# Layer normalisation over channels on partitions: GpSimd adds the channel halves and the halves of the squares, and the mean squares are kept as eight rows of 128 tokens in batches of two groups

## What is computed

```python
def _ln_t(v, eps=1e-05):
    m = jnp.mean(v, axis=-1, keepdims=True)
    s = jnp.var(v, axis=-1, keepdims=True)
    return (v - m) / jnp.sqrt(s + eps)

def layer_norm(x, g, b):
    m = jnp.mean(x, axis=-1, keepdims=True)
    v = jnp.mean(jnp.square(x - m), axis=-1, keepdims=True)
    return (x - m) * jax.lax.rsqrt(v + EPS) * g + b
```

## Time and profile before

| | |
|---|---|
| time before, median of 3 runs | 5374.98 us (5358.56 to 5387.59) |
| profiled execution, its own time | 5375.21 us |
| its span, first to last instruction | 5373.4 us |
| mean granted TensorE clock over the span | 0.892 of full speed |
| busy: TensorE matmul, VectorE, ScalarE, GpSimd | 84%, 55%, 40%, 15% |
| the seven normalisation stages together | 337.90 us |

### The profile page before, as it was taken

How to read it: one execution, slowest core, us unless ns; L and a number is a source line. 1 busy time by engine, 2 the same in 40 slices (tenths; PEclk the granted TensorE clock), 3 DMA queues, 4 the chain that set the end, 5 groups by cost and what they waited for, 6 DMA issues and landing times. The chain is left out here.

```text
span 5373.4 us, 139944 instructions
## 1 busy us (share of the span) xinstructions
PE 4530.5 (84%) x57100; PEld 2834.8 (53%) x57101; DVE 2972.1 (55%) x5849; ACT 2152.0 (40%) x4091; POOL 831.7 (15%) x2139
## 2 busy tenths in 40 slices
PE   3679898887997888897688886799999999984995
PEld 1237777773436777774355554354454545433663
DVE  3444444453024544454488886488686877852343
ACT  1133223232123333331466664277575766721221
POOL 0000000000000000000355553011111111104012
PEclk7788878798998988898899998899999999985997
DMA  1000000000000000000100000000000000006123
GB/s 42 2 7 3 3 3 3 3 3 18 0 0 9 4 3 3 3 4 3 38 1 1 1 1 0 10 1 1 1 0 1 0 1 1 0 3 217 61 84 101
DMA packets 47552, 85.70 MB, mean 16 GB/s; under 512 B 7121, under 2 KB 38129, under 8 KB 46065
## 3 DMA queue, kind: packets, MB, share of 16 engines
q1 hardware_dynamic: 40944, 61.84, 3.3%
q0 software_dynamic: 6144, 16.79, 1.0%
HBM read 45.05 MB, written 33.55 MB: 15 GB/s over the span
## 5 line engine op out<-in xcount | busy, mean ns | idle before, releaser
L1775 PE MATMUL psum<-hm_ex,hm_mix 128*128 128x512 f32 x1024 | 510.4, 621 | 42.3 <-ACT hm_Aq L1855 38.3
L1841 ACT ACTIVATE hm_ex<-psum,hm_nm 128x1024 f32<-128x1024 f32 x256 | 285.6, 1116 | 299.4 <-DVE hm_nm L1899 299.4
L1775 PEld LDWEIGHTS psum<-hm_ex,hm_mix 128*128 128x128 f32 x1024 | 175.6, 191 | 352.5 <-issue 344.8
L1914 DVE COPY hm_A<-psum 128x1024 f32<-128x1024 f32 x256 | 312.9, 1222 | 51.5 <-PE psum L1784 47.9
L1909 DVE TENSOR_SCALAR_CACHE_REDUCE hm_plus<-hm_Aq,hm_cbcol,hm_sums 128x1024 f32<-128x1024 f32 x256 | 340.5, 1330 | 0.0
L1899 DVE TENSOR_REDUCE hm_nm<-psum 128x1 f32<-128x1024 f32 x256 | 311.0, 1215 | 13.5 <-PE psum L1763 13.5
L1784 PEld LDWEIGHTS psum<-K,hm_Aq 128*128 128x128 f32 x2048 | 236.6, 140 | 150.0 <-issue 145.4
L957 DVE TENSOR_TENSOR fw_M<-fw_M,psum 128x256 f32<-128x256 f32 x256 | 107.8, 421 | 348.1 <-PE psum L728 345.6
L1846 ACT ACTIVATE hm_junk<-hm_Aq 128x1024 f32<-128x1024 f32 x256 | 270.6, 1057 | 30.3
L1763 PE MATMUL psum<-hm_kt,hm_qd 64*32 64x512 f32 x4096 | 280.1, 606 | 0.0
L1321 ACT ACTIVATE pt_signs<-pt_acts,pt_tb 128x1024 f32<-128x1024 f32 (+1 forms) x224 | 227.6, 1018 | 116.1 <-POOL pt_tb L1188 95.0
(11 more groups left out here) (379 smaller groups left out, 9044.6 us busy)
## 6 DMA issues: line engine op xcount, KB each, us to landing
ex_rows_in<-ex_zero SPq DMA_DIRECT2D x2, 5120.0 KB, 24.8
ex_xs<-ex_rows_in SPq DMA_DIRECT2D x80, 128.0 KB
ex_rows_out<-ex_ys SPq DMA_DIRECT2D x80, 128.0 KB, 1.7
ex_w<-in_ex_w SPq DMA_DIRECT2D x2, 4096.0 KB
X<-in_x SPq DMA_DIRECT2D x2, 2048.0 KB, 12.5
out_y<-X SPq DMA_DIRECT2D x2, 2048.0 KB, 9.0
ff_w<-in_ff_w SPq DMA_DIRECT2D x2, 1024.0 KB, 5.8
pt_w_proc<-in_pt_proc SPq DMA_DIRECT2D x1, 2048.0 KB, 7.6
```

Source lines behind the costliest of these rows:

```text
L1775: mm = pe.matmul(bank[4 + c], mix[:, u, :], ex[:, u, 512 * c:512 * c + 512], start=True, stop=True)
L1841: act.activation(ex[:, u, :], flat2(psum[:, 2 * u:2 * u + 2, :]), ACT.Exp, bias=nm[:, u:u + 1], accum_out=rsum[:, u:u + 1]).then_inc(s_ex, 1)
L1914: dve.tensor_copy(A[:, :, :, QT_ * t:QT_ * t + QT_], flat2(psum[:, 6:8, :]).rearrange("p (m g n) -> p m g n", m=MT, g=HEADS)).then_inc(s_a ...
```

## The change

GpSimd gets two lists of additions. `sum_halves(g)` adds the two channel halves of the source into one of two buffers `halves`, and `sum_squares(g)` adds the two halves of the squares into one of two buffers `sqs`. TensorE then needs one matmul of 512 columns for a mean instead of two. The mean squares are laid out otherwise: a batch is two groups, 1024 tokens, as a tile of eight rows by 128 tokens. `squares(g)` is four matmuls of 128 columns with weights of eight columns, `spread(g)` four matmuls of 128 columns, each copying one row, and root and reciprocal work on [8, 128] tiles, four times a stage. The lists of all engines become one pipeline over t: group t is centred, t - 2 has its squares summed, t - 4 is spread and scaled. `sq` has two buffers instead of three. The numbers computed are the same up to rounding.

```diff
@@ -338,67 +338,89 @@
     nc = k.nc
-    HALF = NG // 2
+    PARTS = GROUP // P
+    PAIRS = NG // 2
+    ROWS = 2 * PARTS
     with ExitStack() as ctx:
-        sq = k.sb(f"{name}_sq", [P, 3, CH, GROUP], ctx)
-        std = k.sb(f"{name}_std", [HALF, 2, GROUP], ctx)
-        rstd = k.sb(f"{name}_rstd", [HALF, 2, GROUP], ctx)
-        eps = k.sb(f"{name}_eps", [P, 1], ctx)
-        pick = k.sb(f"{name}_pick", [P, 2 * HALF - 1], ctx)
-        s_zero, s_eps, s_mean, s_cen, s_sq, s_msq, s_std, s_rstd, s_bc, s_out, s_shift = (
-            k.sem(f"s_{name}_{n}") for n in "zero eps mean cen sq msq std rstd bc out shift".split())
+        sb = lambda n, s: k.sb(f"{name}_{n}", s, ctx)
+        halves = sb("halves", [P, 2, GROUP])
+        sq = sb("sq", [P, 2, CH, GROUP])
+        sqs = sb("sqs", [P, 2, GROUP])
+        std = sb("std", [ROWS, PAIRS, P])
+        rstd = sb("rstd", [ROWS, PAIRS, P])
+        pick = sb("pick", [P, 2 * ROWS - 1])
+        eps = sb("eps", [P, 1])
+        s_zero, s_eps, s_halves, s_mean, s_cen, s_sq, s_sqs, s_msq, s_std, s_rstd, s_bc, s_out, s_shift = (
+            k.sem(f"s_{name}_{n}") for n in "zero eps halves mean cen sq sqs msq std rstd bc out shift".split())
         bank = k.bank
...
             def _(pool):
+                def sum_halves(g):
+                    if g >= 2:
+                        pool.wait_ge(s_mean, g - 1)
+                    pool.tensor_tensor(halves[:, g % 2, :], at(src, g)[:, 0, :], at(src, g)[:, 1, :],
+                                       ALU.add).then_inc(s_halves, 1)
+
+                def sum_squares(g):
+                    pool.wait_ge(s_sq, g + 1)
+                    if g >= 2:
+                        pool.wait_ge(s_msq, g - 1)
+                    pool.tensor_tensor(sqs[:, g % 2, :], sq[:, g % 2, 0, :], sq[:, g % 2, 1, :],
+                                       ALU.add).then_inc(s_sqs, 1)
+
                 pool.memset(eps[:, :], EPS)
                 pool.memset(pick[:, :], 0.0).then_inc(s_zero, 1)
                 pool.wait_ge(s_zero, 1)
-                pool.memset(pick[:, HALF - 1:HALF], 1.0 / C).then_inc(s_eps, 1)
+                pool.memset(pick[:, ROWS - 1:ROWS], 1.0 / C).then_inc(s_eps, 1)
+                sum_halves(0)
+                sum_halves(1)
+                for g in range(NG):
+                    if g + 2 < NG:
+                        sum_halves(g + 2)
+                    sum_squares(g)
 
             @block.tensor
             def _(pe):
                 def mean(g):
+                    pe.wait_ge(s_halves, g + 1)
                     if g >= 3:
                         pe.wait_ge(s_cen, g - 2)
-                    for h in range(CH):
-                        mm = pe.matmul(bank[g % 3], k.const("ones"), src[:, h, GROUP * g:GROUP * g + GROUP],
-                                       start=(h == 0), stop=(h == CH - 1))
-                    mm.then_inc(s_mean, 1)
+                    pe.matmul(bank[g % 3], k.const("ones"), halves[:, g % 2, :], start=True, stop=True).then_inc(s_mean, 1)
 
                 def squares(g):
-                    pe.wait_ge(s_sq, g + 1)
-                    r = g % HALF
-                    for h in range(CH):
-                        mm = pe.matmul(bank[3 + g // HALF][0:HALF, :], pick[:, HALF - 1 - r:2 * HALF - 1 - r],
-                                       sq[:, g % 3, h, :], start=(r == 0 and h == 0),
-                                       stop=(r == HALF - 1 and h == CH - 1))
+                    pe.wait_ge(s_sqs, g + 1)
+                    if g >= 4 and g % 2 == 0:
+                        pe.wait_ge(s_std, g // 2 - 1)
+                    for q in range(PARTS):
+                        r = PARTS * (g % 2) + q
+                        mm = pe.matmul(bank[3 + g // 2 % 2][0:ROWS, 0:P], pick[:, ROWS - 1 - r:2 * ROWS - 1 - r],
+                                       sqs[:, g % 2, P * q:P * q + P], start=(r == 0), stop=(r == ROWS - 1))
                     mm.then_inc(s_msq, 1)
 
                 def spread(g):
-                    pe.wait_ge(s_rstd, g // HALF + 1)
+                    pe.wait_ge(s_rstd, g // 2 + 1)
                     if g >= 3:
                         pe.wait_ge(s_out, g - 2)
-                    r = g % HALF
-                    pe.matmul(bank[5 + g % 3], k.const("ident")[0:HALF, r:r + 1].broadcast_to([HALF, P]),
-                              rstd[:, g // HALF, :], start=True, stop=True).then_inc(s_bc, 1)
-
-                mean(0)
-                mean(1)
+                    for q in range(PARTS):
+                        r = PARTS * (g % 2) + q
+                        mm = pe.matmul(bank[5 + g % 3][:, P * q:P * q + P],
+                                       k.const("ident")[0:ROWS, r:r + 1].broadcast_to([ROWS, P]), rstd[:, g // 2, :],
+                                       start=True, stop=True)
+                    mm.then_inc(s_bc, 1)
+
                 pe.wait_ge(s_eps, 1)
-                for g in range(HALF):
-                    mean(g + 2)
-                    squares(g)
-                mean(6)
-                mean(7)
-                for g in range(HALF):
-                    squares(HALF + g)
-                    spread(g)
-                for g in range(HALF):
-                    spread(HALF + g)
+                for t in range(NG + 4):
+                    if t < NG:
+                        mean(t)
+                    if 0 <= t - 2 < NG:
+                        squares(t - 2)
+                    if 0 <= t - 4 < NG:
+                        spread(t - 4)
...
                 def square(g):
                     act.wait_ge(s_cen, g + 1)
-                    if g >= 3:
-                        act.wait_ge(s_msq, g - 2)
-                    act.activation(sq[:, g % 3, :, :], at(dst, g), ACT.Square).then_inc(s_sq, 1)
+                    if g >= 2:
+                        act.wait_ge(s_sqs, g - 1)
+                    act.activation(sq[:, g % 2, :, :], at(dst, g), ACT.Square).then_inc(s_sq, 1)
 
                 def root(b):
-                    act.wait_ge(s_msq, HALF * b + HALF)
-                    act.activation(std[:, b, :], bank[3 + b][0:HALF, :], ACT.Sqrt,
-                                   bias=eps[0:HALF, :]).then_inc(s_std, 1)
+                    act.wait_ge(s_msq, 2 * b + 2)
+                    act.activation(std[:, b, :], bank[3 + b % 2][0:ROWS, 0:P], ACT.Sqrt,
+                                   bias=eps[0:ROWS, :]).then_inc(s_std, 1)
...
-                for g in range(HALF + 1):
-                    square(g)
-                root(0)
-                for g in range(HALF + 1, NG):
-                    square(g)
-                root(1)
-                for g in range(NG):
-                    move(g)
+                for t in range(NG + 5):
+                    if t < NG:
+                        square(t)
+                    if t >= 3 and t % 2 == 1 and t // 2 <= PAIRS:
+                        root(t // 2 - 1)
+                    if 0 <= t - 5 < NG:
+                        move(t - 5)
...
                 def scale(g):
                     dve.wait_ge(s_bc, g + 1)
-                    dve.wait_ge(s_cen, g + 1)
+                    dve.wait_ge(s_sq, g + 1)
...
-                for g in range(HALF + 2):
-                    centre(g)
-                invert(0)
-                centre(6)
-                centre(7)
-                for g in range(HALF):
-                    scale(g)
-                invert(1)
-                for g in range(HALF, NG):
-                    scale(g)
+                for t in range(NG + 4):
+                    if t < NG:
+                        centre(t)
+                    if t >= 3 and t % 2 == 1 and t // 2 <= PAIRS:
+                        invert(t // 2 - 1)
+                    if 0 <= t - 4 < NG:
+                        scale(t - 4)
                 dve.wait_ge(s_out, NG)
```

## The result

The changed kernel takes 5393.4 us (median of 20 runs, 5360.1 to 5424.2) against 5362.3 of the kernel before on the same chip (20 runs, 5338.2 to 5394.5): ratio 1.0049, 95% interval 1.003 to 1.0069. The forecast of 5311 us and its range are missed on the slow side. The profiled execution took 5396.4 us, its span is 5394.6.

A forecast was written before the change was run, and what follows sets the result against it. TensorE was taken to bound each normalisation stage. From 5375.2 us, 66.7 saved over the seven stages came off and 2.5 for the configuration load was added, giving 5311 us, range 5280 to 5358.

The forecast's parts named there:

- So a microsecond taken from a stage is one off the total: Seven normalisation stages, 337.90 us together: nothing else runs in them and each ends at a barrier, so savings count fully.
- the last subtraction: Whole kernel: 5375.2 us less 66.7 saved in the seven normalisations, plus 2.5 for the configuration load, gives 5311.
- or if the next stages' lengths change too: Stages behind the normalisations: a change in their lengths was listed as a sign that the prediction is wrong.
- GpSimd's addition: Normalisation stages: each of GpSimd's sixteen additions of 512 columns was priced at 1.26 us.
- The cycle of 3.0: Middle of a normalisation stage: TensorE and VectorE set 3.0 us a group, GpSimd needing 2.5.
- the tail: End of a normalisation stage, after group 7 is summed: last squares, root, reciprocal, spreads and multiplication at half clock, 11.0 us.
- the rival of a tail at full clock: End of a normalisation stage: the clock also stays up there, 3.5 us off a stage, total 5287; chance 0.10.
- The configuration load: Start of ln2: a one-time load now stands ahead of GpSimd's first sum, priced at 2.5 us.
- Half clock in the middle: Normalisation stages: TensorE's clock stays at half, total 5387; chance 0.10 in all stages, 0.08 in some.
- Additions of 1.9: Normalisation stages: each GpSimd addition takes 1.9 us, 3.7 more a stage, total 5337; chance 0.10.
- Mutual blocking: Normalisation stages: GpSimd and VectorE keep each other out, about 56 us a stage, total 5433; chance 0.04.
- The search: Lookup stage: different rounding sets its flag, calling the eighth normalisation and a search, more than 38 us; chance 0.02.

The follow-up runs named there:

- e1_trim: The changed kernel with 8 redundant TensorE waits a normalisation stage left out, putting the fast-weight stages at their old block places; 5285.5 us, ratio 0.983.
- e12_flat: e1_trim with padding matmuls, TensorE's fast-weight loop written out in full and four repeated matmuls in one product of each tile; 5056.6 us, ratio 0.946.
- e5_pad: e1_trim with 16 one-column matmuls after the convolution stage's last matmul and 8 ahead of the feed-forward stage's first wait; 5260.1 us, ratio 0.990.
- e10_bpad: The kernel before with 54 one-column matmuls after the convolution stage's last matmul and 4 ahead of the feed-forward stage's first wait; 5239.6 us, ratio 0.982.

## Why the prediction was wrong

**The step that failed** is "So a microsecond taken from a stage is one off the total", and with it the last subtraction, 5375.2 less 66.7. It holds for the barriers and not for the program's text: 136 more TensorE instructions in each stage shifted everything behind them against the 256-instruction blocks, and the two fast-weight stretches grew by 111.2 us. The text named the sign ("or if the next stages' lengths change too") and no mechanism; none of the rivals was this one. With the true saving, 5375.2 - 86.8 would be 5288, and e1_trim, with that saving (its seven stages are 252.0 us) and the old places, measured 5285.5 (four runs, 5268.9 to 5327.0, on a chip where the kernel before took 5370.8). That the two agree within 3 us is in part luck.

**The prices, term by term.** GpSimd's addition: 1.26 us forecast, 1.267 and 1.268 measured (L373, L366). The reciprocal of [8, 128]: 0.95, measured 0.941. First subtraction 3.8 us into ln2: 201.15 - 197.31 = 3.8. The squares of group 3 summed at 15.0: 14.9. The cycle of 3.0: L393 starts at 211.98, 215.09 and 218.20, so 3.1. Group 7 summed at 27.0: 26.3. The mis-sized term is the tail, 11.0 against 8.5 (26.3 to 34.86): squares(7) and a spread still ran on full clock, which fell at 226.6 only. ln2 by clock:

```profile
197.31:202.00 4.69, 2.94 (x4) 1.12 (x4) 0.85 (x1) 0.20 (x1) 3.53 (x6) 0.50 0.00 0
202.00:226.60 24.60, 21.62 (x125) 12.73 (x124) 17.42 (x17) 9.56 (x12) 16.53 (x14) 0.99 0.00 1
226.60:232.17 5.57, 4.04 (x18) 3.48 (x17) 4.00 (x4) 0.00 (x0) 0.00 (x0) 0.50 0.00 0
```

That is between the forecast and the rival of a tail at full clock. Over the seven stages the sum was 20.1 us short: 9.4 in ln2, ln3 and ln4 (38.0 forecast; 34.9, 35.0 and 34.8 measured), 2.1 in ln5, 8.6 in the stages with gain (40.0 forecast; 38.0, 37.1 and 36.4 measured), which were not taken apart. The configuration load, priced at 2.5, cost nothing to be seen: it stands at 197.6 and the first addition starts at 197.67.

**The rivals.** Half clock in the middle: 0.99 there, so no. Additions of 1.9: no. Mutual blocking: VectorE's L462 takes 1.204 us beside GpSimd, 1.208 before; no. The search: the eighth normalisation does not show among the stages.

## What to carry to other kernels

A change that adds or removes instructions on an engine with a long loop moves all code behind it against the instruction blocks, so compare the stages that the diff does not touch, tile by tile, before judging it by the total. Look for idle time put down to "issue" that stands at the same record of every pass: here it drifted by a fixed count from pass to pass, as a block boundary does, and redundant waits or a few tiny matmuls moved it to a place where it cost nothing. Try an edit at two places within a block, or its worth (here the 86.8 us of the normalisations, 1.6%) can read as nothing.

## What the runs showed that was not expected

- The late block stops TensorE for about 1 to 2 us, a jump back in its loop for about 3 to 7. Where half clock follows, it holds for 3 to 24 us of the tile and costs more than the stop: the tile with the jump takes 30 to 35 us against 22.5.
- A fast-weight stretch is the longer the more of it runs at half clock: 997 us with 464 at half (layer 1, changed), 900 with 224 (layer 1, before), 802 with 65 (layer 0, e12_flat).
- The Trainium skill, page "Runtime: NRT & Kernel Launch", section "Instruction fetch mechanics", calls the cost of a block boundary mostly hidden, and warns of a taken branch. Both are seen here: of five boundaries in a tile mostly one shows, and the jump shows every time. Why that one is late stays open; the stops looked at stand among 32x32 matmuls and weight loads, whose records start 0.01 us apart or less (45 of them from 2074.50 to 2074.67 in the tile above), while the packet ahead of this stop takes 1.38 us. That the clock falls because of the stop was not tried by itself: spells came behind stops and went when the stops went, but many stops had no spell behind them.
- From ln5's end to the end of the span took 535 to 537 us in some runs and 498 to 501 in e5_pad to e10_bpad, whatever the kernel; so kernels that were not timed together are compared by their ratios to the kernel before. What differs there was not looked into.
